# A bias load, four small stores and the high halves of the rows, moved between queues and turns

## The reference, cut to what matters

```python
def _L1_ffn_ref(x, gate_w, w1, b1, w2, b2):      # x: 4096 tokens of 256
    gate_logits = x_flat @ gate_w.T               # 8 experts
    topk_vals, topk_idx = jax.lax.top_k(gate_logits, 2)
    topk_w = jax.nn.softmax(topk_vals, axis=-1)
    ...
    for e in range(8):
        h = jax.nn.gelu(x_flat @ w1[e].T + b1[e], approximate=False)   # 1024 wide
        y = h @ w2[e].T + b2[e]
        out = out + comb[:, e:e + 1] * y
...
t = t + _L1_ffn_ref(_ln_t(t), ...)                # tokens normalised first
```

## Time and profile before

| | us |
|---|---|
| median of three runs | 1466.11 |
| the profiled execution, its own time | 1467.59 |
| its span, first to last instruction | 1465.5 |
| TensorE busy (share of the span) | 1213.9 (83%) |
| VectorE, ScalarE, POOL busy | 797.0, 695.7, 601.7 |
| routing, from the first instruction of the stage to the last turn's choice | 922.62 to 973.19 |
| plan, to POOL's first index copy | to 1010.17 |
| experts, from TensorE's first matmul | 1020.15 to the end |

### The profile page before, as it was taken

The page is one execution under the profiler, slowest core; times in us unless marked ns, Lnnn a source line. Parts: engine busy times, 40 slices in busy tenths (PEclk is TensorE's granted clock), DMA queues, the critical chain, the costliest instruction groups (busy, mean ns, idle before and its releaser), DMA issues. The chain is left out here.

```text
span 1465.5 us, 28035 instructions
## 1 busy us (share of the span) xinstructions
PE 1213.9 (83%) x9389; PEld 822.9 (56%) x9390; DVE 797.0 (54%) x1573; ACT 695.7 (47%) x1344; POOL 601.7 (41%) x490
## 2 busy tenths in 40 slices
PE   3979989834798799778987987842999999999993
PEld 1546657622234433443344334741888888888882
DVE  3865655444546574666567444771545454545451
ACT  3565444426667566756675664322333323232321
POOL 3977645210730083008000000102477777777761
PEclk7999999977899999989999999555999999999997
DMA  5755887941981298139604830795343444444437
GB/s 172 171 133 141 173 191 169 189 108 24 210 244 41 53 224 233 39 72 241 178 1 83 192 100 15 254 362 143 53 80 73 80 72 74 75 80 72 77 56 243
DMA packets 334344, 190.20 MB, mean 130 GB/s; under 512 B 277872, under 2 KB 314992, under 8 KB 332080
## 3 DMA queue, kind: packets, MB, share of 16 engines
q1 hardware_dynamic: 297040, 133.50, 38.1%
q0 software_dynamic: 24704, 54.34, 16.2%
q10 hardware_dynamic: 12512, 1.21, 0.8%
HBM read 64.85 MB, written 60.96 MB: 86 GB/s over the span
## 5 line engine op out<-in xcount | busy, mean ns | idle before, releaser
L2115 ACT ACTIVATE all_last_rows<-moe_hbank,moe_b1T 128x256 f32<-128x256 f32 x312 | 129.8, 472 | 268.1 <-PE moe_hbank L2026 259.7
L2026 PE MATMUL moe_hbank<-moe_rowT,l_w1T 128*128 128x256 f16 x1872 | 213.1, 275 | 11.2 <-DMA moe_rowT<-moe_ends 11.2
L2041 PE MATMUL moe_ybank<-l_w2T,moe_shared 128*128 x1872 | 210.6, 273 | 0.0
L2026 PEld LDWEIGHTS moe_hbank<-moe_rowT,l_w1T 128*128 x1872 | 184.3, 99 | 33.9 <-issue 11.5
L2041 PEld LDWEIGHTS moe_ybank<-l_w2T,moe_shared 128*128 128x128 f16 x1872 | 183.2, 98 | 21.2
L1175 ACT ACTIVATE block_probs<-block_bank 128x1024 f32<-128x1024 f32 (+1 forms) x192 | 144.5, 808 | 75.2 <-PE block_bank L937 62.6
L1955 POOL DMA_INDIRECT acc_scratch<-moe_ends,moe_whither x78 | 132.4, 1698 | 78.5 <-issue 49.3
L804 POOL COPY block_stack<-block_stack 128x512 f16<-128x512 f16 x16 | 10.6, 664 | 364.6 <-ACT block_stack L1159 364.6
L2291 DVE TENSOR_SCALAR moe_shared<-all_last_rows 128x2048 f16<-128x2048 f32 x39 | 48.1, 1234 | 172.3 <-ACT all_last_rows L2115 168.3
L1928 POOL DMA_INDIRECT moe_ends<-rows_scratch,moe_which x78 | 120.8, 1549 | 45.2 <-POOL moe_which L1924 31.7
L934 PE MATMUL block_bank<-block_qkT 128*128 128x512 f16 (+3 forms) x384 | 95.1, 335 | 46.2 <-issue 24.3
(11 more groups left out here) (365 smaller groups left out, 2539.5 us busy)
## 6 DMA issues: line engine op xcount, KB each, us to landing
front_raw<-in_L_ffn_w POOLq DMA_DIRECT2D x32, 512.0 KB, 5.0
w_turned<-block_qk SPq DMA_DIRECT2D x32, 512.0 KB, 3.7
w_parts<-front_raw_hi POOLq DMA_DIRECT2D x32, 256.0 KB, 5.1
w_parts<-front_raw_lo POOLq DMA_DIRECT2D x32, 256.0 KB, 5.8
l_w1T<-w_turned SPq DMA_DIRECT2D x8, 1024.0 KB, 11.2
l_w2T<-w_turned SPq DMA_DIRECT2D x8, 1024.0 KB, 12.7
front_shared<-in_x SPq DMA_DIRECT2D x8, 512.0 KB, 7.0
x_scratch<-conv_mixed SPq DMA_DIRECT2D x8, 512.0 KB, 3.9
```

Of the source, the lines that this page charges most:

```text
L2026: last = pe.matmul(hbank[:, c, :], w1T[:, e, wp, k, c * P:(c + 1) * P], rowT[q][:, xp * CC + k, :], start=n == 0, stop=n == 5)
L2041: last = pe.matmul(ybank[q][:, t, :], (hid_hi, hid_lo)[hp][q][:, c, t * P:(t + 1) * P], w2T[:, e, wp, c, :], start=n == 0, stop=n == 3 * H ...
L2115: act.activation(hid[:, c, :], hbank[:, c, :], ACT.Gelu, bias=b1T[:, e, c:c + 1], scale=1.0 / (GAIN * GAIN)).then_inc(S["gelu_done"], 1)
```

## The change

Three things are moved; no arithmetic is added or removed.

- The first bias `b1T` gets its own buffer and semaphore outside the stage and is loaded by SP's queue in `token_block`, as the last of `gate_loads`. ScalarE waits for `b1_loaded` before the experts, VectorE for the second bias alone.
- `store_extra(a - 1)` goes from after tile 5 of turn `a` to after tile 7. The last one goes from the first round of the plan to right after the last exponential, and the last `token_weights` on VectorE goes from the first round of the one-hot tables to before `group_bases`.
- The high halves are made in two instructions of four tiles each (`x_high`): those of turn 0 after tiles 1 and 3 of turn 0, those of turn `a + 1` after tiles 5 and 7 of turn `a`.

```diff
+                def x_high(a, half):
+                    ts = slice(half * PER // 2, (half + 1) * PER // 2)
+                    act.wait_ge(S["x_done"], a * PER + ts.stop)
+                    if a >= 2 and half == 0:
+                        act.wait_ge(S[f"x_stored{a % 2}"], 16)
+                    act.activation(xrow[a % 2][:, ts, 0:D], tok[a][:, ts, :], ACT.Copy, scale=GAIN).then_inc(S["x_hi"], 1)
...
-                        if a and i == 6:
-                            store_extra(a - 1)
...
-                        if i == 1:
-                            act.wait_ge(S["x_done"], (a + 1) * PER)
-                            if a >= 2:
-                                act.wait_ge(S[f"x_stored{a % 2}"], 16)
-                            act.activation(xrow[a % 2][:, :, 0:D], tok[a][:, :, :], ACT.Copy, scale=GAIN).then_inc(S["x_hi"], 1)
+                        if a == 0 and i in (1, 3):
+                            x_high(0, i // 2)
+                        if a + 1 < TURNS and i in (5, 7):
+                            x_high(a + 1, i // 2 - 2)
+                    if a:
+                        store_extra(a - 1)
                 exps(TURNS - 1)
-                act.dma_start(b1T[:, :, :], b1.rearrange("e (c p) -> p e c", p=P), allow_slow_non_contiguous=True).then_inc(S["bias_loaded"], 16)
+                store_extra(TURNS - 1)
...
-                    if a == 0:
-                        store_extra(TURNS - 1)
...
-                act.wait_ge(S["bias_loaded"], 32)
+                act.wait_ge(b1_loaded, 16)
...
-                    dve.wait_ge(S["x_hi"], a + 1)
+                    dve.wait_ge(S["x_hi"], 2 * (a + 1))
...
+                token_weights(TURNS - 1)
                 done, upto = group_bases()
...
-                    if a == 0:
-                        token_weights(TURNS - 1)
...
-                dve.wait_ge(S["bias_loaded"], 32)
+                dve.wait_ge(S["bias_loaded"], 16)
...
+        b1T, b1_loaded = s.sb("b1T", [P, E_N, HC]), s.sem("b1_loaded")
...
+        gate_loads.append((b1T[:, :, :], p["L1_ffn_b1"].rearrange("e (c p) -> p e c", p=P), b1_loaded))
```

More of the change, by code:

```diff
@@ L1729, with route_and_experts @@
 TURNS = 4
-def route_and_experts(nc, acc, rows, ident, gT, gate_loaded, w1_turned, w2_turned, b1, b2, w1T, w2T, w_loaded, expert_of, carried, out):
+def route_and_experts(nc, acc, rows, ident, gT, gate_loaded, w1_turned, w2_turned, b1T, b1_loaded, b2, w1T, w2T, w_loaded, expert_of, carried, out):
     PER = TILES // TURNS
@@ L1760, in route_and_experts @@
         y = [ends[:, 4 * GT * ROW + i * 2 * GT * D:4 * GT * ROW + (i + 1) * 2 * GT * D].bitcast(F32).rearrange("p (t d) -> p t d", t=GT) for i in range(2)]
-        b1T = s.sb("b1T", [P, E_N, HC])
         work = s.sb("work", [P, E_N * D])
@@ L2393, in build @@
             w_loaded = s.sem("w_loaded")
-            route_and_experts(nc, acc, rows, ident, gT, gate_loaded, w1_turned, w2_turned, p["L1_ffn_b1"], p["L1_ffn_b2"],
+            route_and_experts(nc, acc, rows, ident, gT, gate_loaded, w1_turned, w2_turned, b1T, b1_loaded, p["L1_ffn_b2"],
                               w1T, w2T, w_loaded, expert_of, carried, out)
```

## The result

| | before | after |
|---|---|---|
| median of five runs each, us | 1468.82 (1464.83 to 1472.41) | 1453.18 (1449.62 to 1456.06) |
| ratio | 1 | 0.9899, 95% interval 0.9875 to 0.9923 |
| span of the profiled execution | 1465.5 | 1446.8 |
| routing, first VectorE instruction, to the first expert matmul ("the stage") | 97.5 | 81.7 |
| first expert matmul to the end | 445.4 | 445.0 |

The kernel is faster by 1.0%, which on 1466.11 us is 14.8 us (11.3 to 18.3); 16.3 had been forecast. The two spans differ by 18.7 us, but 15.8 of that lies in the stage.

A forecast was written before the change was run, and what follows sets the result against it. The start of POOL's first gather, held by `slots` and small stores, was taken to bound the kernel. 14.08 + 3.76 - 0.38 brought `slots` 17.46 us earlier, the gather 16.3: 1466.11 - 16.3 = 1449.8 us, range 1446.8 to 1453.8.

The forecast's parts named there:

- The bias and the rounds: With the bias off ScalarE's queue, VectorE's fourth one-hot round follows the first by 10.74 us, not 24.82: 14.08 us gained.
- The turns: Moved small stores and split high halves remove TensorE's waits for copies: 1.02 us in turn 0, 2.74 in turns 1 and 2.
- Close, but free: In turn 2, ScalarE reaches turn 3's high half just after turn 1's row store lands; a miss costs under 0.5 us.
- What is late next: POOL's first gather waits for the fourth small store, landing at 993.8 after the weights end at 992.5: 16.3 us gained.
- Bounds: Gather gain between 17.5 us, if `slots` is last, and 12.9, if the weights don't move and landing takes 1.85.
- The token block: The bias load on SP's queue takes 3.6 us, covered by 47 us of idle SP before the transposes: no cost.
- Rival 1: Fourth store and gather hang on a weight stream that doesn't move: gain 12.9 to 14 us, 1452.1 to 1453.2; chance 0.20.
- Rival 2: `slots` comes last, as the small store passes more than one packet per weight packet: gain 17.5, 1448.6 us; chance 0.20.
- Rival 3: The bias holds SP's queue in the token block, delaying transposes: 95 us lost, about 1545 us; chance 0.03.
- Rival 4: The small store on ScalarE stalls even without the bias, queued behind the weights: about 1463 us; chance 0.04.
- Wrong: Signs against: token-block transpose after 361, ScalarE waiting for the row store in turn 2, first gather before 993 or after 996.
- Right: Signs for: no long ScalarE DMA issue, rounds 3.6 us apart, gather near 994 within 2 us of the weights' end.

The follow-up runs named there:

- change_again: The changed kernel, unaltered, run and profiled a second time on the same chip as later runs: 1452.80 us, 0.9892 of before.
- bias_only: The kernel before with only the bias load moved to SP's queue in the token block: 1455.62 us, 0.9892 of before.
- bias_back: The changed kernel with the bias load back on ScalarE's queue, behind the last small store: 1454.85 us (three of four runs), 0.9893 of before.
- turns_only: The changed kernel with bias load, last token weights and last small store put back as before; only the turns changed: 1465.56 us, 0.9968 of before.
- last_on_pool: The changed kernel with the last small store issued by POOL on its own queue: 1450.53 us, 0.9873 of before.
- bias_x16: The changed kernel with the bias loaded sixteen times in the token block, into sixteen buffers: 1484.62 us (one run).

## Where the prediction held and which step failed, point by point

The time came out close to the forecast. The step that fixes the start of the first gather failed all the same: two errors in it pulled against each other.

**The bound** was right. The stage lost 15.8 us in the first profile and 16.3 in the second (change_again), and from the first expert matmul on nothing moved (445.4, 445.0).

**The bias and the rounds**, 14.08 us forecast: 14.10 measured (24.82 - 10.72). bias_only shows the part by itself. The reason given, an issue that waits for the drain of the queue, is right for `before`; told as "the next DMA" in the expectation of bias_back it was too narrow, and that forecast missed by it.

**The weights ahead of the count**, a cost of 0.38 us: the count comes 4.26 us after the last choice instead of 3.84, so 0.42.

**The turns**, 3.76 us forecast: the last choice came 47.04 - 42.63 = 4.41 us earlier. This term was too small. Turn 0 gave 1.18 for 1.02, turn 1 1.70 for 1.39, turn 2 1.37 for 1.35 and turn 3 0.16 for none. Each turn with the whole high half inside is 0.16 us longer, which I had seen as no wait in the rows. Against it stands a wait that the prediction had called "Close, but free": ScalarE waited 0.47 us for the row store, in other executions up to 1.41. The bound given for it, under 0.5 us, was wrong as well: with the wait of 1.41 us (turns_only) turn 2 lasted 11.45 us against 10.21 without a wait, so it cost 1.2.

**What is late next.** The kind was right: the gather waits for the fourth small store, and that for the weights. The gap in the weight stream closed as forecast (share 0.96 to 1.09 in every microsecond from 948 to 954). The step that failed is the tail behind the weights, "the rest takes 0.5 us, and its landing another 0.8 us", and with it "That is 993.8, 1.1 us after `slots`". Not 1.3 but 3.0 us passed from the fall of the rate (989.0) to the landing (992.0), and the gather came 2.8 us after `slots` in one profile and 2.7 in the other. The landing itself was not mis-sized: it came 0.6 us after the start of the store's last packet. The rest of the store was: its last packet came 2.4 us after the fall, and its sixteen steps of completion are spread from 989.71 to 991.97. I read that as DMA engines that don't end together.

The trace of `before` has the same tail. Its last weight packet starts at 996.3, 1.4 us after the 994.9 that the prediction took for the end. And the 1.85 us in "Bounds" was no landing time: the third store's last 32-byte packet started at 989.6, and it landed 0.7 us after that; the rest of the 1.85 was the same unevenness.

Against this error stands another. The fall of the rate came 3.4 us earlier in the stage and not 2.4. The last weight packet came 2.9 us earlier (70.7 us into the stage for 73.7), as much as SP's store of turn 2's rows (30.3 for 33.2) and as the gain of turns 0 and 1 (2.9 for 2.4 forecast); turns_only moves it by 2.7 us and bias_only not at all. So the term on the turns, too small, did reach the sum by way of the weights. In all the gather came 0.8 us later in the stage than forecast (72.0 for 71.2); from the gather to the first matmul it was 9.6 us instead of 10.0, which leaves 0.5 us on 16.3. That so little is left is luck. last_on_pool takes the wait for the store away and gives 2.5 to 2.6 us back between `slots` and the gather.

**The token block**, nothing: the transposes start where they did. By bias_x16 a load takes 5.3 us rather than 3.6, still far from 47.

**Rivals.** Rival 1 (12.9 to 14 us) rests on weights that don't move; they moved. Rival 2 (`slots` last) is out by 2.8 us of waiting. Rival 3 is out for one load; sixteen show that the transposes wait for the queue. Rival 4 (the store stalls without the bias) is out by bias_only.

The Trainium skill's figure of 2.0 us for the fixed part of a DMA (DMA: Bandwidth & Descriptors, "Anatomy of one DMA — SWDGE (gpsimd) path") would have given a gain of 15.1. The 15.8 measured lie between that and 16.3, but not for the page's reason: the landing took 0.6 us after the last packet, and the rest of the tail was the store's own last packets, which came late.

**The signs.** Three of the signs given under "Wrong" appeared as they were written: a transpose after 361 (364.64), a first gather before 993 (992.21) and ScalarE's wait for the row store. The first two were given on the clock of one trace, and in the other what stands ahead had shifted: by landmarks the transpose came 0.2 us later after the block's start, and the gather, 72.0 us into the stage, would stand at 994.7 on the clock of `before`. The third is real, 0.47 us. Of the signs under "Right" one failed: the gather came 3.2 us after the fall of the weights' rate and not within 2 (1.3 after the last weight packet started).

**The time.** The median of the changed kernel was 1453.18, near the upper end of the range, partly because the paired runs of `before` were slower too, 1468.82 for 1466.11; by the ratio it would be 1451.3 against a forecast of 1449.8. It also happens to be the time of rival 1 (1452.1 to 1453.2); only the stage, 15.8 us shorter and not 12.9 to 14, and the weights that moved tell the two apart.

## What to carry to other kernels

A long idle stretch of a compute engine that begins with a DMA issue can be a full queue, as it was here: look at what stands ahead in the same queue and what the other queues are moving, and take the load with many tiny pieces to a time when nothing else moves. Then look for the next store that a gather waits for, and give it a queue where it isn't behind others and goes in few packets. For its landing count with the last packets of the stream beside it, not with the moment when the rate falls. Where several waits stand one behind the other, each that is taken away gives back only what the next one leaves. Count in landmarks of the stage when runs scatter by more than the effect.

## What the runs showed of the hardware

- Two hardware queues shared the DMA engines packet by packet: 288 small packets against 288 weight packets in 5 us, so a store of 1024 pieces of 32 bytes, 1024 packets there, took 24.9 us to land on ScalarE's queue. The same store on POOL's queue went in 32 packets and landed in 5.9 us beside the same weights.
- The issue of the 8192-piece load took 0.45 us with nothing ahead of it in its queue, 0.41 us behind most of one small store, 13.29 us behind two, and 5.26 us each when sixteen followed one another with next to nothing else moving.
- The end of a stream isn't sharp: the last weight packet started 1.9 us after the rate had fallen (1.4 in `before`), and the small store beside it completed in sixteen steps over 2.3 us, where one with nothing beside it took 0.4. The last small store on ScalarE's queue landed 0.3 to 0.9 us after the start of its last packet in all eight profiles that have it there.
